# Packing two row blocks of w2 into each unit of the ternary weight passes, with the packed stores issued from SP

## The chip, the cores and the metric

The kernel runs on all 8 cores of one Trainium2 chip. Every core runs the same program on its own half of one sequence. The time is the device time of the slowest core in microseconds.

## What is computed

A layer in two parts, for x of shape (4, 4096, 1024). The first is a gated linear recurrence with projections and a layer norm. The second, which the change touches, is a feed-forward part with ternary weights ("bit linear") and a depthwise convolution of width 3 between its two products:

```python
def weight_quant(w):
    scale = 1.0 / jnp.clip(jnp.mean(jnp.abs(w)), 1e-05)
    return jnp.clip(jnp.round(w * scale), -1, 1) / scale

h = bit_linear(x, w1)                      # w1 (4096, 1024)
h = depthwise_conv1d(h.transpose(0, 2, 1), conv_w, conv_b)
h = jax.nn.silu(h.transpose(0, 2, 1))
return bit_linear(h, w2)                   # w2 (1024, 4096)
x = _layernorm(x + attn(x)); x = _layernorm(x + ffn(x))
```

So each weight matrix is read twice before it can be used: once for the mean of its absolute values, once to be scaled, rounded and clipped to -1, 0 or 1.

## The kernel before

Each core works on 2052 tokens (its 2048 and two on each side) in three stages that barriers separate (lines 665 and 1014).

Stage A prepares. Lines 336 to 415 fold the gate weights (`wtr`, `ps_pre`, `G`). The gate loop from line 574 then goes over all 4096 tokens in 16 slices of 256: SP loads `xgf` (1 MB in pieces of 1 KB, two buffers), ScalarE makes the high bf16 part `xgh`, GpSimd the low part `xgl`, TensorE does 24 matmuls into `ps_g`, and ScalarE writes three gate activations into `g80` (lines 601, 605, 609; `g` in the trace). A scan on VectorE (lines 636 and 641) gives the states.

The ternary work is woven into this stage. `tern_pass1` (line 437) takes a weight in units: a unit is a block of 128 rows by up to TW = 2048 columns in float32. w1, stored as (1024, 4096), gives 16 units of 1 MB. w2, stored as (4096, 1024), gives 32 units of 0.5 MB. Each unit is loaded by SP into one of four buffers `twf0` to `twf3`. Even units are summed by ScalarE (line 447), odd ones by VectorE (line 452). `pump_p1(9)` (line 612) advances this by nine units at the end of each gate slice, and since every engine runs its instructions in the order of the program, the loads of nine units stand ahead of the next slice's `xgf` on SP, and the sums stand between two slices' activations on ScalarE.

`tern_pass2` (line 486) runs after the scan, in the same units and buffers, w1 first. Of an even unit ScalarE makes `tu` (line 521, scaled), VectorE `tk16` (line 525, clamped to a 16-bit integer, `tk` in the trace), ScalarE `tb` (line 528, bf16). Of an odd unit VectorE makes `tu` and `tk16` (lines 532, 536) and ScalarE `tb` (line 539). There are two `tb` buffers. The store of `tb` to `w1q_hbm` or `w2q_hbm` is issued by ScalarE's queue, since that is the default of `store`:

```python
def load(dst_ap, src_ap, region, q="SP", reads=()):
def store(dst_ap, src_ap, reads, region, q="ACT"):
```

Waits come from `finalize_and_emit` (line 54): each operation names the regions that it reads and writes, and the engine waits, ahead of the instruction and in its own order, for the semaphores of the last writer and of the readers. A load into `twf0` therefore waits for whoever read `twf0` last, and a store waits for the cast that wrote its `tb`.

After the scan the kernel emits `tern_p2_all()` (line 662) and a barrier. Stage B (from line 667) first loads W_in, W_D and W_out in 24 pieces of 0.5 MB through two buffers `xb0` and `xb1`, with rows of 4 KB as those of w2, splits them in bf16 parts, then runs the projections (`ps_a`). Stage C is the feed-forward part (`ps_m`, `ps_o`), which reads `w1q_hbm` and `w2q_hbm`.

Of the kernel before, what the change touches and what calls it, by code (L numbers as in the profile page):

```python
# [184 lines left out]
def build_nc(debug=False):  # L185
    nc = bass.Bass("TRN2", target_bir_lowering=False)
    p = Prog(nc)
    V, A, PE, GP, SY = nc.vector, nc.scalar, nc.tensor, nc.gpsimd, nc.sync
# [53 lines left out]
    def load(dst_ap, src_ap, region, q="SP", reads=()):  # L242
        p.op(q, lambda d=dst_ap, s=src_ap, e=QENG[q]: e.dma_start(out=d, in_=s),
             reads=reads, writes=(region,), dma=True)

    def store(dst_ap, src_ap, reads, region, q="ACT"):
        p.op(q, lambda d=dst_ap, s=src_ap, e=QENG[q]: e.dma_start(out=d, in_=s),
             reads=reads, writes=(region,), dma=True)
# [32 lines left out]
    TW = 1024 if SAFE_ROUND else 2048  # L281
# [54 lines left out]
    for fc in range(8):  # L336
# [3 lines left out]
        for j in range(8):  # L340
# [6 lines left out]
             writes=(f"G{fc}",))  # L347
# [82 lines left out]

    twfs, tus, tk16s, tbs, tk, trr, tcp, tcol = alloc_tern(stA)

    def tern_slices(nrows, width):
        return [(rc, c0, min(width, c0 + TW))
                for rc in range(nrows) for c0 in range(0, width, TW)]

    def tern_pass1(src, nrows, width, mean_out, mean_rg, tg,
                   ps_hbuf, ps_rg, scol):
        stag = f"tcol{scol}"
        slices = tern_slices(nrows, width)  # L440
        for i, (rc, c0, c1) in enumerate(slices):
            wv = c1 - c0
            pr = i % NTB
            twf, tu = twfs[pr], tus[pr]
            load(twf[:, 0:wv], src[rc * 128:(rc + 1) * 128, c0:c1], f"twf{pr}")
            if i % 2 == 0:
                p.op("ACT", lambda twf=twf, tu=tu, e=wv: A.activation(
                    tu[:, 0:e], twf[:, 0:e], AF.Abs, accum_out=tcol[:, 0:1]),
                     reads=(f"twf{pr}",), writes=(f"tu{pr % 2}", "tcol0"))
                acc, arg = "tcol0", 0  # L450
            else:
                p.op("DVE", lambda twf=twf, e=wv: V.tensor_reduce(
                    tcol[:, 3:4].rearrange("p (t o) -> p t o", o=1),
                    twf[:, 0:e].rearrange("p (t e) -> p t e", t=1),
                    AX, OP.add, apply_absolute_value=True),
                     reads=(f"twf{pr}",), writes=("tcol3",))
                acc, arg = "tcol3", 3
            if i == 0:
                p.op("DVE", lambda: V.tensor_copy(tcol[:, 1:2], tcol[:, 0:1]),
                     reads=(acc,), writes=("tcol1",))  # L460
            else:
                p.op("DVE", lambda a=arg: V.tensor_add(tcol[:, 1:2],
                                                       tcol[:, 1:2],
                                                       tcol[:, a:a + 1]),
                     reads=(acc, "tcol1"), writes=("tcol1",))
            yield
        p.op("DVE", lambda: V.tensor_scalar(tcol[:, 1:2], tcol[:, 1:2],
                                            1.0 / (nrows * 128 * width), None,
                                            OP.mult),
             reads=("tcol1",), writes=("tcol1",))  # L470
        mm("parsum" + tg, ps_hbuf[0:1, 0:1], s_onesc[:], tcol[:, 1:2],
           reads=("s_onesc", "tcol1"), wr=ps_rg, start=True, stop=True)
        p.op("DVE", lambda: V.tensor_copy(tcol[0:1, 1:2], ps_hbuf[0:1, 0:1]),
             reads=(ps_rg,), writes=("tcol1",))
        mm("parbc" + tg, ps_hbuf[0:128, 0:1], s_ones1[:], tcol[0:1, 1:2],
           reads=("s_ones1", "tcol1"), wr=ps_rg, start=True, stop=True)
        p.op("DVE", lambda: V.tensor_copy(tcol[:, 1:2], ps_hbuf[0:128, 0:1]),
             reads=(ps_rg,), writes=("tcol1",))
        p.op("DVE", lambda: V.tensor_scalar_max(mean_out[:], tcol[:, 1:2], 1e-5),
             reads=("tcol1",), writes=(mean_rg,))  # L480
        p.op("DVE", lambda mo=mean_out, sc=scol: V.reciprocal(
            tcol[:, sc:sc + 1], mo[:]),
             reads=(mean_rg,), writes=(stag,))
        yield

    def tern_pass2(src, dst_hbm, nrows, width, tg, scol):
        stag = f"tcol{scol}"
        slices = tern_slices(nrows, width)
        for i, (rc, c0, c1) in enumerate(slices):
            wv = c1 - c0  # L490
            pr = i % NTB
            twf, tu, tk16, tb = twfs[pr], tus[pr], tk16s[pr], tbs[pr]
            load(twf[:, 0:wv], src[rc * 128:(rc + 1) * 128, c0:c1], f"twf{pr}")
            if SAFE_ROUND:
                p.op("DVE", lambda twf=twf, tu=tu, e=wv: V.tensor_scalar(
                    tu[:, 0:e], twf[:, 0:e], tcol[:, scol:scol + 1], None,
                    OP.mult),
                     reads=(f"twf{pr}", stag), writes=(f"tu{pr % 2}",))
                p.op("DVE", lambda tu=tu, e=wv: V.tensor_copy(tk[:, 0:e],
                                                              tu[:, 0:e]),  # L500
                     reads=(f"tu{pr % 2}",), writes=("tk",))
                p.op("DVE", lambda tu=tu, e=wv: V.tensor_sub(trr[:, 0:e],
                                                             tu[:, 0:e],
                                                             tk[:, 0:e]),
                     reads=(f"tu{pr % 2}", "tk"), writes=("trr",))
                p.op("DVE", lambda e=wv: V.tensor_scalar(tcp[:, 0:e], trr[:, 0:e],
                                                         0.5, None, OP.is_gt),
                     reads=("trr",), writes=("tcp",))
                p.op("DVE", lambda tu=tu, e=wv: V.scalar_tensor_tensor(
                    tu[:, 0:e], trr[:, 0:e], -0.5, tcp[:, 0:e], OP.is_lt,  # L510
                    OP.subtract),
                     reads=("trr", "tcp"), writes=(f"tu{pr % 2}",))
                p.op("DVE", lambda tu=tu, e=wv: V.tensor_sub(tu[:, 0:e],
                                                             tk[:, 0:e],
                                                             tu[:, 0:e]),
                     reads=(f"tu{pr % 2}", "tk"), writes=(f"tu{pr % 2}",))
                p.op("DVE", lambda tu=tu, tb=tb, e=wv: V.tensor_scalar(
                    tb[:, 0:e], tu[:, 0:e], 1.0, -1.0, OP.min, OP.max),
                     reads=(f"tu{pr % 2}",), writes=(f"tb{pr % 2}",))
            elif i % 2 == 0:  # L520
                p.op("ACT", lambda twf=twf, tu=tu, e=wv: A.activation(
                    tu[:, 0:e], twf[:, 0:e], AF.Identity,
                    scale=tcol[:, scol:scol + 1]),
                     reads=(f"twf{pr}", stag), writes=(f"tu{pr % 2}",))
                p.op("DVE", lambda tu=tu, tk16=tk16, e=wv: V.tensor_scalar(
                    tk16[:, 0:e], tu[:, 0:e], 1.49, -1.49, OP.min, OP.max),
                     reads=(f"tu{pr % 2}",), writes=(f"tk16{pr % 2}",))
                p.op("ACT", lambda tk16=tk16, tb=tb, e=wv: A.activation(
                    tb[:, 0:e], tk16[:, 0:e], AF.Copy),
                     reads=(f"tk16{pr % 2}",), writes=(f"tb{pr % 2}",))  # L530
            else:
                p.op("DVE", lambda twf=twf, tu=tu, e=wv: V.tensor_scalar(
                    tu[:, 0:e], twf[:, 0:e], tcol[:, scol:scol + 1], 1.49,
                    OP.mult, OP.min),
                     reads=(f"twf{pr}", stag), writes=(f"tu{pr % 2}",))
                p.op("DVE", lambda tu=tu, tk16=tk16, e=wv: V.tensor_scalar(
                    tk16[:, 0:e], tu[:, 0:e], -1.49, None, OP.max),
                     reads=(f"tu{pr % 2}",), writes=(f"tk16{pr % 2}",))
                p.op("ACT", lambda tk16=tk16, tb=tb, e=wv: A.activation(
                    tb[:, 0:e], tk16[:, 0:e], AF.Copy),  # L540
                     reads=(f"tk16{pr % 2}",), writes=(f"tb{pr % 2}",))
            store(dst_hbm[rc * 128:(rc + 1) * 128, c0:c1], tb[:, 0:wv],
                  (f"tb{pr % 2}",), f"q{tg}{rc}_{c0}")
            yield

    def tern_p1_all(ps_hbuf, ps_rg):
# [1056 lines left out]
```

How the kernel before makes its waits and increments, by code:

```python
                def body(handle, eng=eng, idxs=idxs):  # L164
                    for i in idxs:
                        o = ops[i]
                        for sh, val in waits_l[i]:
                            handle.wait_ge(sh, val)
                        instr = o["fn"]() if o["fn"] is not None else handle.nop()
                        if o["sem"] is not None:
                            instr.then_inc(o["sem"][1], 16 if o["dma"] else 1)
                    if eng == "SP":
                        for e2 in ENGINES:
                            if cnt.get(e2, 0):
                                handle.wait_ge(chain[e2], cnt[e2])
                        for j in range(NDMA):
                            if dcnt[j]:
                                handle.wait_ge(dpool[j], dcnt[j])
```

## Time and profile before

| what | us |
|---|---|
| median of three runs | 2483.28 (2475.99 to 2513.78) |
| the profiled execution, its own time | 2478.09 |
| its span, slowest core | 2476.6 |
| spans of all eight cores | 2451.3 to 2476.6 |
| pass 1 of both weights, within the gate slices | about 123 to 303 |
| pass 2 of w1, then of w2 | 459 to 551, 551 to 648 |
| first matmul of stage B | 756 |

The span is the time from the first instruction to the last on one core; the execution's own time is 1.5 us more. Times in the rows below count from the span's start. A row of instructions gives busy time and the idle time of the engine just before, with what ended it. "SPq" and "ACTq" are the queues' issues of a transfer. "Landing" is from the issue of a transfer to its completion.

### The profile page before, as it was taken

How to read it: one execution, taken by the hardware profiler on the slowest of the kernel's cores; microseconds unless marked ns; L12 is line 12 of the kernel's file. 1: busy time of each engine (PE TensorE's matmuls, PEld its weight loads, DVE VectorE, ACT ScalarE, POOL GpSimd, SP SyncE). 2: the span in 40 equal slices, each digit the busy share in tenths (PEclk: the TensorE clock that was granted, in tenths of full speed). 3: DMA queues.
4: the chain of work that ended last, by engine and by line, in shares of the span. 5: the costliest groups of instructions: out<-in, count | busy, mean ns of one | idle time of the engine just before them, and what ended most of it. 6: DMA issues, size and time to landing. Idle time of an engine off the chain costs nothing.

```text
span 2476.6 us, 30490 instructions; the slowest of 8 cores (2451.3 to 2476.6 us)
## 1 busy us (share of the span) xinstructions
PE 1343.5 (54%) x9255; PEld 965.8 (39%) x9255; DVE 1086.4 (44%) x2418; ACT 870.8 (35%) x1552; POOL 194.9 (8%) x78
## 2 busy tenths in 40 slices
PE   6712234000007786786886882056658568576566
PEld 6711133000006665665665762034335344343332
DVE  1123300433212433434334334278787787776852
ACT  0023322255311222122222221066465474574551
POOL 0011132000250001001001001000000000000000
PEclk9975566555558988998998986588879889788788
DMA  4385632587542101101100001450110110111000
GB/s 127 101 267 192 220 85 56 182 282 261 169 131 48 39 26 44 39 35 47 40 35 31 22 22 43 159 161 1 29 48 18 34 52 18 35 38 31 26 35 26
DMA packets 132968, 201.71 MB, mean 81 GB/s; under 512 B 46184, under 2 KB 95465, under 8 KB 127624
## 3 DMA queue, kind: packets, MB, share of 16 engines
q1 hardware_dynamic: 114120, 144.92, 20.0%
q10 hardware_dynamic: 18688, 54.85, 6.1%
q8 instruction: 78, 1.28, 0.2%
q14 instruction: 82, 0.67, 0.1%
HBM read 152.52 MB, written 38.03 MB: 77 GB/s over the span
## 4 chain that ended last, share of the span: by engine, by line
PE 35%; DVE 21%; DMA 15%; ACT 13%; issue 8%; POOL 6%; SPq 2%; ACTq 1%; DVEq 1%; POOLq 0%
PE ps_a L261 16%; PE ps_o L261 8%; DVE pmax L1337 5%; PE ps_m L261 4%; PE ps_g L261 3%; DMA xgf<-xg_fm 3%; POOL xgl L584 3%; DMA w2q_hbm<-tb 2%; DMA w1q_hbm<-tb 2%; PE ps_pre L261 2%; ACT sc_a L1088 2%; DVE hbuf L1311 2%; DVE sc_a L1106 2%; POOL xtm L893 2%; DMA wtr<-W_B_T 1%
## 5 line engine op out<-in xcount | busy, mean ns | idle before, releaser
L261 PE MATMUL ps_a<-pA_h,Win_hi 128*128 128x256 bf16 (+1 forms) x512 | 149.2, 291 | 403.9 <-ACT pA_h L739 329.5
L261 PE MATMUL ps_m<-r1qg,w1q 128*128 128x258 bf16 (+2 forms) x2304 | 301.9, 275 | 109.4 <-DVE hbuf L1311 69.6
L261 PE MATMUL ps_o<-w2q,hq_b 128*128 128x512 bf16 (+1 forms) x1088 | 288.6, 402 | 43.8 <-DVE ps_s L1433 23.6
L261 PEld LDWEIGHTS ps_m<-r1qg,w1q 128*128 128x128 bf16 x2304 | 212.8, 102 | 213.4 <-issue 147.2
L1088 ACT ACTIVATE sc_a<-hbuf,s_convb,s_convw 128x256 f32<-128x256 f32 (+2 forms) x288 | 166.1, 577 | 339.6 <-DVE hbuf L1311 319.2
L261 PEld LDWEIGHTS ps_a<-pA_h,Win_hi 128*128 128x128 bf16 x512 | 52.8, 103 | 420.8 <-issue 411.5
L261 PE MATMUL ps_a<-pB_h,WD_hi 128*128 128x256 bf16 (+1 forms) x512 | 148.4, 290 | 56.8 <-ACT pB_h L765 37.7
L261 PEld LDWEIGHTS ps_o<-w2q,hq_b 128*128 128x128 bf16 (+1 forms) x1088 | 106.5, 101 | 149.4 <-issue 67.7
L261 PE MATMUL ps_a<-pA_l,Win_hi 128*128 128x256 bf16 (+1 forms) x512 | 148.9, 291 | 6.9 <-DVE pA_l L743 6.9
L1311 DVE SCALAR_TENSOR_TENSOR hbuf<-ps_m,dqs 128x258 f32<-128x258 f32 (+2 forms) x288 | 113.1, 393 | 86.8 <-PE ps_m L261 81.7
L261 PE MATMUL ps_a<-pB_l,WD_hi 128*128 128x256 bf16 (+1 forms) x512 | 148.2, 289 | 1.1 <-DVE pB_l L769 1.1
L261 PE MATMUL ps_a<-pA_h,Win_lo 128*128 128x256 bf16 (+1 forms) x512 | 148.3, 290 | 0.0
L261 PE MATMUL ps_a<-pB_h,WD_lo 128*128 128x256 bf16 (+1 forms) x512 | 147.5, 288 | 0.0
L261 PE MATMUL ps_a<-pA_h,Wout_hi 128*128 128x256 bf16 (+1 forms) x512 | 139.4, 272 | 2.8 <-DVE zS L829 2.8
L261 PE MATMUL ps_a<-pA_l,Wout_hi 128*128 128x256 bf16 (+1 forms) x512 | 139.5, 272 | 0.0
L261 PE MATMUL ps_a<-pA_h,Wout_lo 128*128 128x256 bf16 (+1 forms) x512 | 139.0, 272 | 0.0
L1106 DVE SCALAR_TENSOR_TENSOR sc_a<-hbuf,s_convw,sc_a 128x256 f32<-128x256 f32 (+2 forms) x288 | 129.0, 448 | 15.9 <-ACT sc_a L1088 15.5
L1094 ACT ACTIVATE sc_d<-hbuf,s_convw 128x256 f32<-128x256 f32 (+2 forms) x288 | 135.5, 471 | 0.1
L261 PE MATMUL ps_g<-xgh,WG_hi 128*80 128x256 bf16 x128 | 51.6, 403 | 143.3 <-ACT xgh L580 143.3
L1114 DVE TENSOR_TENSOR sc_d<-sc_d,sc_a 128x256 f32<-128x256 f32 (+2 forms) x288 | 114.1, 396 | 30.6 <-DVE sc_a L1106 0.5
L1337 DVE TENSOR_REDUCE pmax<-hbuf 128x256 f32<-128x8192 f32 (+1 forms) x9 | 124.1, 13787 | 0.4 <-ACT hbuf L1118 0.4
L1118 ACT ACTIVATE hbuf<-sc_d 128x256 f32<-128x256 f32 (+2 forms) x288 | 112.8, 392 | 5.4 <-DVE sc_d L1114 4.7
(196 smaller groups left out, 2318.6 us busy)
## 6 DMA issues: line engine op xcount, KB each, us to landing
twf<-w1t_f SPq DMA_DIRECT2D x32, 1024.0 KB, 10.7
twf<-w2t_f SPq DMA_DIRECT2D x64, 512.0 KB, 5.4
xgf<-xg_fm SPq DMA_DIRECT2D x16, 1024.0 KB, 7.6
wtr<-W_B_T SPq DMA_DIRECT2D x16, 512.0 KB, 4.3
w1q_hbm<-tb ACTq DMA_DIRECT2D x16, 512.0 KB, 6.0
w2q_hbm<-tb ACTq DMA_DIRECT2D x32, 256.0 KB, 3.7
xtm<-x_tm ACTq DMA_DIRECT2D x16, 512.0 KB, 3.3
r_hbm<-z_tm ACTq DMA_DIRECT2D x16, 512.0 KB, 2.6
```

Source lines behind the costliest of these rows:

```text
L261: PE.matmul(o, l, r, start=st, stop=sp),
L584: GP.tensor_sub(xgl[:], xgf[:], xgh[:]),
L893: p.op("GP", lambda e=uw: GP.tensor_add(xtm[0:e, :], xtm[0:e, :], s_betb[0:e, :]), reads=("xtm", "s_betb"), writes=("xtm",))
L1088: A.activation(sc_as[mm_ % 2][:, 0:e], h[:, c0:c0 + e], AF.Identity, bias=s_convb[:, mm_:mm_ + 1], scale=s_convw[:, 32 + mm_:33 + mm_]),
L1094: A.activation(sc_ds[mm_ % 2][:, 0:e], h[:, c0 + 1:c0 + 1 + e], AF.Identity, scale=s_convw[:, 64 + mm_:65 + mm_]),
L1106: V.scalar_tensor_tensor(sc_as[mm_ % 2][:, 0:e], h[:, c0 - 1:c0 - 1 + e], s_convw[:, mm_:mm_ + 1], sc_as[mm_ % 2][:, 0:e], OP.mult, OP.add),
L1114: V.tensor_add(sc_ds[mm_ % 2][:, 0:e], sc_ds[mm_ % 2][:, 0:e], sc_as[mm_ % 2][:, 0:e]),
L1118: A.activation(h[:, c0:c0 + e], sc_ds[mm_ % 2][:, 0:e], AF.Silu),
L1311: V.scalar_tensor_tensor(o, i, 1.0, d, OP.mult, OP.mult),
L1337: p.op("DVE", lambda e=fw, c0=co: V.tensor_reduce(pmax[:, 0:e].rearrange("p (t o) -> p t o", o=1), hbuf[:, :].rearrange("p (c t) -> p t c" ...
```

## The change

`tern_slices` is replaced by `tern_units`. For w1 (4096 wide) nothing is different: a unit is 128 rows by 2048 columns. For w2 (1024 wide) a unit now has two blocks of 128 rows side by side in the buffer, 128 x 2 x 1024, so that both passes go over 16 units of 1 MB where there were 32 of 0.5 MB. All operations on such a unit are 2048 wide. Its load is one transfer of 1 MB in rows of 4 KB. Its store is one transfer of 0.5 MB in rows of 2 KB, and it is issued by SP (line 469 of the changed kernel), in the order of the program: behind the load of the same unit and ahead of the load of the next. The stores of w1 stay on ScalarE's queue.

```diff
--- before.py
+++ after.py
@@ -430,19 +430,53 @@
-    def tern_slices(nrows, width):
-        return [(rc, c0, min(width, c0 + TW))
-                for rc in range(nrows) for c0 in range(0, width, TW)]
+    def tern_units(srcT, nrows, width, tg, dstT=None):
+        units = []
+        if width >= TW:
+            for rc in range(nrows):
+                for c0 in range(0, width, TW):
+                    c1 = min(width, c0 + TW)
+                    sap = srcT[rc * 128:(rc + 1) * 128, c0:c1]
+                    dap = (None if dstT is None
+                           else dstT[rc * 128:(rc + 1) * 128, c0:c1])
+                    units.append((sap, dap, c1 - c0, None,
+                                  (f"q{tg}{rc}_{c0}",)))
+        else:
+            g = TW // width
+            for r0 in range(0, nrows, g):
+                ge = min(g, nrows - r0)
+                sap = srcT[r0 * 128:(r0 + ge) * 128, :].rearrange(
+                    "(c p) t -> p c t", p=128)
+                dap = (None if dstT is None
+                       else dstT[r0 * 128:(r0 + ge) * 128, :].rearrange(
+                           "(c p) t -> p c t", p=128))
+                units.append((sap, dap, ge * width, ge,
+                              tuple(f"q{tg}{r}_0" for r in range(r0, r0 + ge))))
+        return units
+
+    def tern_load(buf, sap, wv, gpack, region):
+        if gpack is None:
+            load(buf[:, 0:wv], sap, region)
+        else:
+            d3 = buf[:, 0:wv].rearrange("p (c t) -> p c t", c=gpack)
+            load(d3, sap, region)
+
+    def tern_store(buf, dap, wv, gpack, tags, rdtag):
+        if gpack is None:
+            store(dap, buf[:, 0:wv], (rdtag,), tags[0])
+        else:
+            s3 = buf[:, 0:wv].rearrange("p (c t) -> p c t", c=gpack)
+            p.op("SP", lambda d=dap, b=s3: SY.dma_start(out=d, in_=b),
+                 reads=(rdtag,), writes=tags, dma=True)
...
-        slices = tern_slices(nrows, width)
-        for i, (rc, c0, c1) in enumerate(slices):
-            wv = c1 - c0
+        units = tern_units(src, nrows, width, tg)
+        for i, (sap, dap, wv, gpack, tags) in enumerate(units):
             pr = i % NTB
             twf, tu = twfs[pr], tus[pr]
-            load(twf[:, 0:wv], src[rc * 128:(rc + 1) * 128, c0:c1], f"twf{pr}")
+            tern_load(twf, sap, wv, gpack, f"twf{pr}")
...
-            store(dst_hbm[rc * 128:(rc + 1) * 128, c0:c1], tb[:, 0:wv],
-                  (f"tb{pr % 2}",), f"q{tg}{rc}_{c0}")
+            tern_store(tb, dap, wv, gpack, tags, f"tb{pr % 2}")
             yield
```

(`tern_pass2` takes its units and its load in the same way as `tern_pass1`.)

SP's order in pass 2 of w2, before; a name's number is that of the buffer, and what stands in brackets are the semaphores that the engine waits for (`ch_ACT` and `ch_DVE` are the compute semaphores of ScalarE and VectorE, `dma...` those of transfers):

```order
L243 DMA twf3<-w2t_f 128x1024 [waits dma22,ch_DVE]
L243 DMA twf0<-w2t_f 128x1024 [waits dma24,ch_ACT]
L243 DMA twf1<-w2t_f 128x1024 [waits dma26,ch_DVE]
L243 DMA twf2<-w2t_f 128x1024 [waits dma28,ch_ACT]
L243 DMA twf3<-w2t_f 128x1024 [waits dma30,ch_DVE]
L243 DMA twf0<-w2t_f 128x1024 [waits dma0,ch_ACT]
```

And now:

```order
L243 DMA twf1<-w2t_f 128x2x1024
L469 DMA w2q_hbm<-tb1 128x2x1024 [waits ch_ACT]
L243 DMA twf2<-w2t_f 128x2x1024
L469 DMA w2q_hbm<-tb0 128x2x1024 [waits ch_ACT]
L243 DMA twf3<-w2t_f 128x2x1024
L469 DMA w2q_hbm<-tb1 128x2x1024 [waits ch_ACT]
L243 DMA twf0<-w2t_f 128x2x1024
L469 DMA w2q_hbm<-tb0 128x2x1024 [waits ch_ACT]
```

Each load was followed by the next load, four ahead. Now a store that waits for ScalarE stands between each load and the next, and the load itself has no wait of its own left.

ScalarE's order at the start of pass 2 of w2, before:

```order
L521 ACTIVATE tu0<-twf0,tcol 128x1024 [waits dma24]
L528 ACTIVATE tb0<-tk16_0 128x1024 [waits dma21,ch_DVE]
L247 DMA w2q_hbm<-tb0 128x1024 [waits ch_ACT]
L539 ACTIVATE tb1<-tk16_1 128x1024 [waits dma23,ch_DVE]
L247 DMA w2q_hbm<-tb1 128x1024 [waits ch_ACT]
L521 ACTIVATE tu0<-twf2,tcol 128x1024 [waits dma28]
L528 ACTIVATE tb0<-tk16_0 128x1024 [waits dma25,ch_DVE]
```

And now (lines 554, 561 and 572 are the former 521, 528 and 539):

```order
L554 ACTIVATE tu0<-twf0,tcol 128x2048 [waits dma8]
L561 ACTIVATE tb0<-tk16_0 128x2048 [waits dma5,ch_DVE]
L572 ACTIVATE tb1<-tk16_1 128x2048 [waits dma7,ch_DVE]
L554 ACTIVATE tu0<-twf2,tcol 128x2048 [waits dma12]
L561 ACTIVATE tb0<-tk16_0 128x2048 [waits dma9,ch_DVE]
```

The two stores in each pair are gone from its queue, and `tu` and `tb` are 2048 wide.

SP's order in pass 1, from the first unit of w2 to the second `xgf` after it, before and now:

```order
L243 DMA twf0<-w2t_f 128x1024 [waits dma0,ch_ACT]
L256 DMA xgf0<-xg_fm 128x8x256
L243 DMA twf1<-w2t_f 128x1024 [waits dma1,ch_DVE]
L243 DMA twf2<-w2t_f 128x1024 [waits dma2,ch_ACT]
L243 DMA twf3<-w2t_f 128x1024 [waits dma3,ch_DVE]
L243 DMA twf0<-w2t_f 128x1024 [waits dma4,ch_ACT]
L243 DMA twf1<-w2t_f 128x1024 [waits dma6,ch_DVE]
L243 DMA twf2<-w2t_f 128x1024 [waits dma7,ch_ACT]
L243 DMA twf3<-w2t_f 128x1024 [waits dma8,ch_DVE]
L243 DMA twf0<-w2t_f 128x1024 [waits dma9,ch_ACT]
L243 DMA twf1<-w2t_f 128x1024 [waits dma10,ch_DVE]
L256 DMA xgf1<-xg_fm 128x8x256
```

```order
L243 DMA twf0<-w2t_f 128x2x1024 [waits dma0,ch_ACT]
L256 DMA xgf0<-xg_fm 128x8x256
L243 DMA twf1<-w2t_f 128x2x1024 [waits dma1,ch_DVE]
L243 DMA twf2<-w2t_f 128x2x1024 [waits dma2,ch_ACT]
L243 DMA twf3<-w2t_f 128x2x1024 [waits dma3,ch_DVE]
L243 DMA twf0<-w2t_f 128x2x1024 [waits dma4,ch_ACT]
L243 DMA twf1<-w2t_f 128x2x1024 [waits dma6,ch_DVE]
L243 DMA twf2<-w2t_f 128x2x1024 [waits dma7,ch_ACT]
L243 DMA twf3<-w2t_f 128x2x1024 [waits dma8,ch_DVE]
L243 DMA twf0<-w2t_f 128x2x1024 [waits dma9,ch_ACT]
L243 DMA twf1<-w2t_f 128x2x1024 [waits dma10,ch_DVE]
L256 DMA xgf1<-xg_fm 128x8x256
```

The order is the same, with units of twice the size. Before, 22 units were left after these; now 6 are.

## Rows read from the trace of the kernel before

**Rows 1.** The page, part 4 (chain by line) and part 5 (costliest groups)

```profile
PE ps_a L261 16%; PE ps_o L261 8%; DVE pmax L1337 5%; PE ps_m L261 4%; PE ps_g L261 3%; DMA xgf<-xg_fm 3%; POOL xgl L584 3%; DMA w2q_hbm<-tb 2%; DMA w1q_hbm<-tb 2%; PE ps_pre L261 2%; ACT sc_a L1088 2%; DVE hbuf L1311 2%; DVE sc_a L1106 2%; POOL xtm L893 2%; DMA wtr<-W_B_T 1%
...
L261 PE MATMUL ps_a<-pA_h,Win_hi 128*128 128x256 bf16 (+1 forms) x512 | 149.2, 291 | 403.9 <-ACT pA_h L739 329.5
```

**Rows 2.** Busy time by stretch (start:end, then its length), pass 1, pass 2, stage B loads

```profile
core 5: us, PE busy (x) PEld busy (x) DVE busy (x) ACT busy (x) POOL busy (x), PEclk, DMA share, GB/s
...
147.90:188.80 40.90, 5.50 (x24) 4.34 (x24) 14.01 (x15) 13.34 (x15) 4.06 (x1) 0.54 0.82 282
188.80:217.20 28.40, 5.87 (x28) 4.82 (x28) 13.36 (x17) 10.47 (x12) 4.05 (x1) 0.58 0.64 222
...
271.90:299.30 27.40, 4.92 (x24) 4.02 (x24) 6.00 (x12) 7.90 (x12) 4.05 (x1) 0.56 0.81 268
299.30:314.90 15.60, 6.20 (x28) 4.95 (x28) 3.75 (x11) 5.55 (x10) 4.05 (x1) 0.54 0.24 68
314.90:326.90 12.00, 4.65 (x24) 3.82 (x24) 0.00 (x0) 3.26 (x4) 4.05 (x1) 0.61 0.25 64
459.00:544.30 85.30, 0.00 (x0) 0.00 (x0) 25.66 (x22) 42.77 (x22) 0.00 (x0) 0.50 0.91 291
551.00:648.10 97.10, 0.00 (x0) 0.00 (x0) 32.80 (x48) 51.84 (x48) 0.00 (x0) 0.50 0.75 246
648.10:756.00 107.90, 0.15 (x1) 0.10 (x1) 12.23 (x13) 13.39 (x15) 50.86 (x24) 0.50 0.50 131
```

**Rows 3.** The chain in order of time, end of pass 2 (start, length, what)

```profile
632.78 5.15 DMA w2q_hbm<-tb
638.07 1.07 ACT tb L528
...
646.04 2.03 DMA w2q_hbm<-tb
```

**Rows 4.** SP's own waits between 551 and 648 us (total, times, longest)

```profile
SPq L168 <- ACT tu L521: 58.3, 14, 5.2
SPq L168 <- DVE tu L532: 14.0, 14, 1.0
```

**Rows 5.** Instructions in order of time, an odd unit of w1, then an even one

```profile
493.54 1.28 DVE L532 TENSOR_SCALAR tu<-twf,tcol 128x2048 f32<-128x2048 f32 x1
...
498.23 0.33 ACTq L247 DMA_DIRECT2D w1q_hbm<-tb  x1
...
542.18 2.00 ACT L521 ACTIVATE tu<-twf,tcol 128x2048 f32<-128x2048 f32 x1 [0.51 <-ACT tb L539]
544.26 2.86 SPq L243 DMA_DIRECT2D twf<-w2t_f  x2
...
545.61 1.91 ACT L528 ACTIVATE tb<-tk 128x2048 bf16<-128x2048 int16 x1 [1.43 <-DVE tk L525]
...
547.60 0.33 ACTq L247 DMA_DIRECT2D w1q_hbm<-tb  x1
548.13 1.91 ACT L539 ACTIVATE tb<-tk 128x2048 bf16<-128x2048 int16 x1 [0.62 <-DVE tk L536]
```

**Rows 6.** DMA issues with size and median us to landing: pass 2, weight loads, page

```profile
twf<-w1t_f SPq DMA_DIRECT2D x16, 1024.0 KB, 10.7
...
twf<-w2t_f SPq DMA_DIRECT2D x28, 512.0 KB, 5.1
...
xb<-W_D SPq DMA_DIRECT2D x8, 512.0 KB, 4.4
xb<-W_in SPq DMA_DIRECT2D x6, 512.0 KB, 4.1
...
r_hbm<-z_tm ACTq DMA_DIRECT2D x16, 512.0 KB, 2.6
```

**Rows 7.** Tile xgf between 320 and 420 us, one 1 MB load at a time

```profile
DMA to landing us min/median/max: 5.6/7.0/7.6
```

**Rows 8.** The chain in order of time, a 512 KB weight load of stage B

```profile
655.80 3.74 DMA xb<-W_in
```

More of the change, by code:

```diff
@@ L487, in tern_pass2 @@
         stag = f"tcol{scol}"
-        slices = tern_slices(nrows, width)
-        for i, (rc, c0, c1) in enumerate(slices):
-            wv = c1 - c0
+        units = tern_units(src, nrows, width, tg, dstT=dst_hbm)
+        for i, (sap, dap, wv, gpack, tags) in enumerate(units):
             pr = i % NTB
             twf, tu, tk16, tb = twfs[pr], tus[pr], tk16s[pr], tbs[pr]
-            load(twf[:, 0:wv], src[rc * 128:(rc + 1) * 128, c0:c1], f"twf{pr}")
+            tern_load(twf, sap, wv, gpack, f"twf{pr}")
             if SAFE_ROUND:
```

## The prediction

> **What bounds the kernel now.** I read the page's chain that ended last first, to see whether the ternary weight work is on it at all: the stores `w2q_hbm<-tb` and `w1q_hbm<-tb` hold 2% of the span each [rows 1]. The costliest group of matmuls then shows what their stage means for TensorE: its first `ps_a` matmul sat 329.5 us behind `pA_h` [rows 1]. In all of that time TensorE does nothing, because the barrier after pass 2 lets no weight of stage B load before the last store of `w2q_hbm` has landed. So a microsecond in pass 2 is a microsecond of the kernel.
>
> Next, busy time by stretch [rows 2]. Pass 2 of w2 takes 97.1 us (551.0 to 648.1) with ScalarE busy 51.8 and VectorE 32.8 and the DMA engines 75%: 16.8 MB in and 8.4 MB out at 246 GB/s. Pass 2 of w1 takes 85.3 us up to 544.3 at 291 GB/s. No engine is full; loads run four buffers ahead. The chain in pass 2 of w2 alternates ScalarE casts with landings of stores [rows 3], which is a loop over the two `tb` buffers with transfers kept in flight. SP's own waits in that stretch are for the reader that frees a `twf` buffer [rows 4], never for the data of a store: those are ACT's.
>
> In pass 1 I cut at the ends of the gate activations: 147.9, 188.8, 217.2, 244.5, 271.9, 299.3, 314.9, 326.9 us. The stretch after a slice's gates, up to the next slice's, took 40.9 us with 9 units of w1 (1 MB each), 28.4 with 7 of w1 and one of w2, 27.4 with 9 of w2 (0.5 MB; there are three of these, the first 27.3), 15.6 with the last four, and 12.0 with none [rows 2].
>
> **The change, part by part.**
>
> Pass 1 of w2: 32 units become 16. The bytes stay. The third and fourth stretch now carry 9 and 6 units of 1 MB, and the fifth and sixth none. I price each by the stretch with about the same bytes, and half a megabyte more at 291 GB/s at 1.8 us: 40.9 + (28.4 + 1.8) + 40.9 + (28.4 + 1.8) + 12.0 + 12.0 = 166.2 us, against 314.9 - 147.9 = 167.0 before. I take 0. Bounds: if half of the added megabytes hid under the matmuls of a slice, the 40.9 us of the third slice would be 27.4, so -13; if the fourth went at the pace of the first (40.9 x 7/9 = 31.8) and the empty ones took 15.6, +8.
>
> Pass 2 of w2, compute: two 1024-wide instructions become one 2048-wide, for the cast 2 x 1.07 us against 1.91 [rows 3, 5]. Over 24 pairs ScalarE saves 24 x 0.23 = 5 us of its 51.8, and it is not what limits. Pass 1 saves 8 such pairs on ScalarE beside transfers: nothing.
>
> Pass 2 of w2, queue: this decides. The store moves from ACT's queue to SP's and stands between the load of its own unit and the load of the next. SP is in order. So behind the waiting store all later loads are queued, and ScalarE waits for these. The load of unit i+1 is issued only when unit i has been loaded, scaled, clamped and cast: the four buffers are of no more use, and one load is in flight at a time. Period of a unit:
>
> (a) from landing to the issue of the store. An even unit of this width: `tu` starts 542.18, store issued 547.60: 5.4 us. An odd one: `tu` starts 493.54, store issued 498.23: 4.7 us [rows 5]. Mean 5.05, taken as 5.1.
>
> (b) SP issues the store, then the load: 0.33 us of issue as in the store's row [rows 5], so the load is issued 0.4 us after the store.
>
> (c) the load, alone in its queue but for the store ahead of it. No row of before has that. From below: 512 KB of the same 4 KB rows took 5.1 us with others in flight, and 4.1 to 4.4 nearly alone [rows 6]. From above: 1 MB amid other loads and stores took 10.7 [rows 6]. Between: 1 MB alone in 1 KB pieces took 5.6 to 7.6, median 7.0 [rows 7]. I build it as 4.3 for the first half megabyte, 1.8 for the second at 291 GB/s, and half of the 1.8 that the store's 512 KB would need ahead of it: 7.0 us.
>
> Period 5.1 + 0.4 + 7.0 = 12.5 us, where before 97.1 / 16 = 6.1 us moved the same megabyte. Start: the first w2 load is issued at 544.26 as now (it waits for unit 12 of w1, [rows 5]); in the tail of w1's traffic I give it 8.3 us, landing at 552.6, after ScalarE is through with w1 (548.13 + 1.91 = 550.0, [rows 5]). Its store is issued 0.1 + 5.4 us later, at 558.1. Fifteen more periods: 745.6. The last store, 512 KB, lands in 2.6 us, as the 512 KB stores of r1 do [rows 6]: 748.2. Now it lands at 646.04 + 2.03 = 648.1 [rows 3]. Loss: 100 us. With (c) at 5.1 the period is 10.6 and the loss 72; with 10.7 it is 16.2 and 156.
>
> What speaks against this is a rule on queues. SP's 58.3 + 14.0 us of waiting on readers [rows 4] show that a wait holds back what is queued behind it, and here the new wait is for the end of a chain. The Trainium skill (DMA: Bandwidth & Descriptors, Issuing engines are not separate DMA queues) says that transfers from SP and ACT share the same 16 engines, and that spreading them over issuers saves only the time to initiate. By that the move would be free. It speaks of transfers; the trace shows what waits ahead of an issue do, and I go by the trace.
>
> A second rule is for larger transfers. In traffic 512 KB took 5.1 us and 1 MB 10.7 [rows 6], so a megabyte costs 10.2 as two and 10.7 as one: nothing is won. The Trainium skill (DMA: Bandwidth & Descriptors, Bandwidth: Measured) advises transfers of at least 1 MiB to reach 75% of peak; with several in flight the trace does not bear out a gain. The same page's fit (Anatomy of one DMA) of 2.0 us plus bytes at 436 GB/s gives, as an estimate, 4.4 us for a lone 1 MB load; with it in (c), and no share for the store, the loss would be 61 us.
>
> Stage B and the FFN: same instructions, later by the same amount. The granted clock is 0.50 all through pass 2 and the weight loads [rows 2], so a longer idle cannot lower it further.
>
> Sum: the profiled execution took 2478.1 us (span 2476.6). 2478.1 + 100 + 0 = 2578. It lies 5.2 below the median of three runs; I add 2 for that: 2580.
>
> **The rivals.**
>
> *Quick loads.* With seven other cores also loading half the time, a lone megabyte lands in 5.1 us: period 10.6, loss 72, time 2550. For: the DMA engines were 75% busy and will be under half. Against: even 512 KB nearly alone took 4.1 to 4.4.
>
> *Slow loads.* The store's writes hold the load behind them in the same queue, and (c) is 10.7 as in traffic: loss 156, time 2634. Against: that row has four loads ahead of it.
>
> *Not slower: the queue does not hold.* If the store's wait kept no load back, the stage would be bound by its transfers. At the 291 GB/s of w1's stretch the 25.2 MB take 86.5 us, 11 less than now: 2467, within 2%. It decides from a period of (648.1 + 50 - 2.6 - 558.1) / 15 = 9.2 us down, that is a load of at most 3.7 us; 3.74 is the shortest I see for half the bytes [rows 8]. Also the queue's order after the change leaves no load to be issued ahead of the wait. So it is nearly excluded.
>
> *Pass 1 moves it.* Its bounds of -13 and +8 widen the range and decide no sign.
>
> **How the numbers follow.** Forecast, a load of 5.5 to 8.6 us: 0.80. Quick loads 0.08, slow loads 0.08, not slower 0.04. A measurement of this kernel tells about 2% (50 us) from no change; the first three cases lie over it, so slower 0.96, within 2% 0.03, faster 0.01 (only the last case, helped by pass 1 and more). Range: load 5.5 gives a period of 11.0 and a loss of 78, with -7 from pass 1: 2550. Load 8.6 gives 14.1 and 124, with +8: 2612.
>
> **What would show it.** In the changed trace: SP waits for ACT `tb` before each of 16 stores, some 12 us each; ScalarE idles before `tu` on a landing of `twf<-w2t_f`, 16 times by about 7 us; landings of these loads in pass 2 near 7 us; DMA share between 552 and 748 near 0.4; the gates end where they do now, within 10 us. The forecast is wrong if two w2 loads are in flight at once in pass 2, if the stage ends before 700, or if the time after it differs by more than 10 us from now.

## The result, and the profile after

The changed kernel takes 2557.3 us in the median of nine runs (2553.4 to 2614.1) against 2485.1 us before (ten runs, 2476.0 to 2548.5). The ratio is 1.030, 95% interval 1.028 to 1.031: slower by some 74 us. Some executions of every kernel here ran slower with one half of the chip at a lower clock (the upper ends of the ranges); the ratios leave them out. Forecast were 2580 us and a range of 2550 to 2612.

The profiled execution took 2559.1 us, its span is 2557.5 us, on core 2 (that of before was on core 5). Answering to [rows 1], the page's chain by line and its costliest group; lines of the file are 32 higher behind the new functions:

```profile
PE ps_a L261 17%; PE ps_o L261 8%; DVE pmax L1369 5%; PE ps_m L261 4%; DMA twf<-w2t_f 4%; PE ps_g L261 3%; DMA xgf<-xg_fm 3%; POOL xgl L616 3%; PE ps_pre L261 2%; DVE sc_a L1138 2%; DMA w1q_hbm<-tb 2%; DVE hbuf L1343 2%; ACT sc_a L1120 2%; DMA wtr<-W_B_T 2%; POOL xtm L925 1%
...
L261 PE MATMUL ps_a<-pA_h,Win_hi 128*128 128x256 bf16 (+1 forms) x512 | 148.3, 290 | 484.6 <-ACT pA_h L771 411.4
```

TensorE now sits 411.4 us behind `pA_h` where it sat 329.5, 82 us more; the loads `twf<-w2t_f` are on the chain with 4%, and `w2q_hbm<-tb`, 2% before, is no longer among the first.

The chain in order of time, in pass 2 of w2 (start, length, what; pieces under 0.1 us left out), which answers to [rows 3]:

```profile
619.13 5.65 DMA twf<-w2t_f
...
624.87 1.30 DVE tu L565
626.27 1.24 DVE tk L569
627.59 1.92 ACT tb L572
629.57 0.37 SPq L469
629.98 6.04 DMA twf<-w2t_f
636.10 2.01 ACT tu L554
638.21 1.24 DVE tk L558
639.53 1.92 ACT tb L561
641.51 0.37 SPq L469
641.92 6.03 DMA twf<-w2t_f
```

This is the whole loop, an odd unit and an even one: load, scale, clamp, cast, issue of the store, next load. Only the landing of the store runs beside it; no two loads are in flight together. From the landing of the odd load (619.13 + 5.65 = 624.78) to the issue of its store are 4.8 us, of the even one (636.02 to 641.51) 5.5; the next load is issued 0.4 us behind the store. The first store was issued at 549.84, the last at 723.81: 15 periods of 11.6 us.

SP's own waits in that stretch, against [rows 4], and the landings (KB, median us), against [rows 6]:

```profile
SPq L168 <- ACT tb L561: 101.2, 8, 22.2
SPq L168 <- ACT tb L572: 80.9, 8, 10.7
```

```profile
twf<-w2t_f SPq DMA_DIRECT2D x15, 1024.0 KB, 5.9
w2q_hbm<-tb SPq DMA_DIRECT2D x15, 512.0 KB, 3.3
```

Sixteen waits for the cast, of 11.4 us each in the mean (a third row of that view is one wait of 2.3 us behind the last store); no reader of a `twf` is waited for any more. Busy time by stretch, against [rows 2]:

```profile
core 2: us, PE busy (x) PEld busy (x) DVE busy (x) ACT busy (x) POOL busy (x), PEclk, DMA share, GB/s
...
188.80:223.20 34.40, 5.39 (x28) 4.43 (x28) 11.13 (x17) 11.32 (x13) 4.06 (x1) 0.55 0.80 274
223.20:259.90 36.70, 5.43 (x24) 4.34 (x24) 10.31 (x12) 11.29 (x13) 4.05 (x1) 0.53 0.77 258
259.90:286.10 26.20, 6.25 (x28) 4.97 (x28) 8.48 (x14) 9.28 (x10) 4.06 (x1) 0.53 0.61 200
286.10:298.20 12.10, 4.67 (x24) 3.84 (x24) 0.00 (x0) 3.30 (x4) 4.05 (x1) 0.61 0.30 87
...
549.80:723.80 174.00, 0.00 (x0) 0.00 (x0) 28.68 (x23) 42.64 (x22) 0.00 (x0) 0.50 0.41 136
```

The DMA engines are at 41% and 136 GB/s, where they were at 75% and 246. In pass 1 the stretches are 40.9, 34.4, 36.7, 26.2, 12.1 and 12.9 us, 163.2 in all against 167.0.

Since the slowest core differs from run to run, I took three lengths on each of the eight cores from the views of the tiles, for every kernel of this study. Medians over the cores, in us: the gates from the first slice's activation to the last slice's (pass 1 lies in it), pass 2 of both weights from the first store of w1q to the first load of W_in, and from there to the end:

| kernel | gates | pass 2 | the rest | ratio to before, 95% interval |
|---|---|---|---|---|
| before | 277.2 | 176.4 | 1820.1 | 1 |
| changed | 270.6 | 257.8 | 1824.8 | 1.030 (1.028 to 1.031) |
| pack_act | 270.6 | 159.8 | 1825.0 | 0.991 (0.988 to 0.994) |
| split_sp | 276.8 | 310.0 | 1822.1 | 1.060 (1.054 to 1.066) |
| pack_sp_ahead | 272.4 | 156.9 | 1822.0 | 0.990 (0.986 to 0.993) |
| wait_only | 272.3 | 258.1 | 1824.8 | 1.032 (1.028 to 1.036) |
| pass1_only | 271.7 | 176.6 | 1820.3 | 0.996 (0.995 to 0.998) |
| pack_act_4tb | 270.6 | 144.6 | 1821.9 | 0.984 (0.982 to 0.985) |
| split_act_4tb | 276.3 | 152.4 | 1820.4 | 0.991 (0.988 to 0.994) |
| load_alone | 269.6 | 279.6 | 1824.5 | 1.041 (1.039 to 1.043) |

The change costs 81 us in pass 2 and gives back 7 in pass 1. The rest is 5 us longer. Each length is from one profiled execution of a kernel, so they do not add up exactly to the 74 us of the ratio.

### The profile page after: what moved, and what is told of

The parts are those of the page before. It is cut to its first block, busy times and chain, and to the rows that moved or that the text cites. A ratio compares the mean times of both kernels' runs of the same rounds, so it can differ in the third digit from the quotient of the medians.

```text
span 2557.5 us, 30049 instructions; the slowest of 8 cores (2527.8 to 2557.5 us)
## 1 busy us (share of the span) xinstructions
PE 1346.0 (53%) x9210; PEld 968.1 (38%) x9255; DVE 1072.9 (42%) x2370; ACT 861.5 (34%) x1512; POOL 194.9 (8%) x78
## 4 chain that ended last, share of the span: by engine, by line
PE 35%; DVE 21%; DMA 16%; ACT 13%; issue 7%; POOL 6%; SPq 2%; DVEq 1%; ACTq 0%; POOLq 0%
PE ps_a L261 17%; PE ps_o L261 8%; DVE pmax L1369 5%; PE ps_m L261 4%; DMA twf<-w2t_f 4%; PE ps_g L261 3%; DMA xgf<-xg_fm 3%; POOL xgl L616 3%; PE ps_pre L261 2%; DVE sc_a L1138 2%; DMA w1q_hbm<-tb 2%; DVE hbuf L1343 2%; ACT sc_a L1120 2%; DMA wtr<-W_B_T 2%; POOL xtm L925 1%
## 5 line engine op out<-in xcount | busy, mean ns | idle before, releaser
L261 PE MATMUL ps_a<-pA_h,Win_hi 128*128 128x256 bf16 (+1 forms) x512 | 148.3, 290 | 484.6 <-ACT pA_h L771 411.4
L261 PE MATMUL ps_o<-w2q,hq_b 128*128 128x512 bf16 (+1 forms) x1043 | 283.3, 405 | 47.4 <-DVE ps_s L1465 23.3
## 6 DMA issues: line engine op xcount, KB each, us to landing
twf<-w1t_f SPq DMA_DIRECT2D x32, 1024.0 KB, 11.4
```

The source lines that it names most:

```text
L261: PE.matmul(o, l, r, start=st, stop=sp),
```

## Experiments

**pack_act: the packing without the move to SP.** The only edit to the changed kernel:

```diff
-            p.op("SP", lambda d=dap, b=s3: SY.dma_start(out=d, in_=b),
+            p.op("ACT", lambda d=dap, b=s3: A.dma_start(out=d, in_=b),
```

> Packed units as in the change, but the packed store is issued by ScalarE's queue as before. Theory A (the loss is SP's wait for the cast, which keeps the next load back): pass 2 of w2 back at 88 to 98 us, pass 1 some 5 us shorter as in the changed kernel, so 0 to 12 us below the kernel before (about 2470 to 2485). Theory B (the packing itself costs, by transfers of 1 MB and less overlap): it stays 40 us or more above before. Theory C (half and half): 20 to 40 above.

Measured: 0.991 of before, some 22 us faster. Pass 2 falls from 257.8 to 159.8, so the move to SP, in this order of loads and stores, costs 98 us. The stores of w2q, by their issues:

```profile
L469 ACTq DMA_DIRECT2D w2q_hbm<-tb x16: 366/366/377, 555.3 to 627.2; - x16
```

(627.2 - 555.3) / 15 = 4.8 us for a unit, against 11.6. Theories B and C are out. The gain was larger than theory A had allowed (12 us at most): packing is worth 17 us in pass 2, which I come back to below.

**split_sp: the move to SP without the packing.** With the first edit every unit of w2 is 0.5 MB again, in both passes; with the second its stores still go by SP:

```diff
-        if width >= TW:
+        if True:
...
-            tern_store(tb, dap, wv, gpack, tags, f"tb{pr % 2}")
+            store(dap, tb[:, 0:wv], (f"tb{pr % 2}",), tags[0],
+                  q="SP" if tg == "w2" else "ACT")
```

> Units of 0.5 MB as before in both passes, but w2's stores are issued by SP between the loads. Theory A: the period of a unit is a chain of about 3.1 us (half widths), 0.4 for SP and a lone load of 4.0 to 4.6 us, so 7.5 to 8.1 us, 32 times: 240 to 260 us for pass 2 of w2 against 97, the kernel about 150 us above before (some 2630). Theory B: no loss, as nothing is packed (within 10 us of before).

Measured: 1.060, some 148 us slower, as theory A had it. Instructions in order of time, one period:

```profile
606.37 0.33 SPq L247 DMA_DIRECT2D w2q_hbm<-tb  x1
606.75 0.42 SPq L243 DMA_DIRECT2D twf<-w2t_f  x1
610.81 1.15 ACT L554 ACTIVATE tu<-twf,tcol 128x1024 f32<-128x1024 f32 x1 [4.51 <-DMA twf<-w2t_f]
...
612.85 1.06 ACT L561 ACTIVATE tb<-tk 128x1024 bf16<-128x1024 int16 x1 [0.89 <-DVE tk L558]
613.97 0.33 SPq L247 DMA_DIRECT2D w2q_hbm<-tb  x1
```

From store to store 7.6 us, with a load landing about 4.1 us after its issue. Half the bytes in each period cost well over half the period. That the packed kernel loses only half as much is thus owed to its packing.

**pack_sp_ahead: stores on SP, behind later loads.** The load of unit i+3 is put ahead of unit i's store; all stores stay on SP:

```diff
-            tern_load(twf, sap, wv, gpack, f"twf{pr}")
+            if tg == "w1":
+                tern_load(twf, sap, wv, gpack, f"twf{pr}")
+            else:
+                for j in (range(0, 4) if i == 0 else (i + 3,)):
+                    if j < len(units):
+                        s_, _, w_, g_, _ = units[j]
+                        tern_load(twfs[j % NTB], s_, w_, g_,
+                                  f"twf{j % NTB}")
```

> Packed, stores on SP, but the load of unit i+3 is put ahead of the store of unit i in the order of the program, so that three or four loads stay in flight. Theory A (the order on SP, not the queue as such): pass 2 of w2 at 88 to 102 us, the kernel within 12 us of before. Theory D (SP as issuer of both, one queue for loads and stores, is the cost): it stays 40 us or more above before.

Measured: 0.990, 25 us faster than before, and as fast as with the stores on ScalarE's queue. The gain was again larger than expected (within 12 us), as in pack_act. Theory D is out: SP can issue both. What is issued in SP's queue:

```profile
563.75 0.37 SPq L469 DMA_DIRECT2D w2q_hbm<-tb  x1
564.16 0.47 SPq L243 DMA_DIRECT2D twf<-w2t_f  x1
566.16 0.37 SPq L469 DMA_DIRECT2D w2q_hbm<-tb  x1
566.57 0.52 SPq L243 DMA_DIRECT2D twf<-w2t_f  x1
571.38 0.37 SPq L469 DMA_DIRECT2D w2q_hbm<-tb  x1
571.79 0.48 SPq L243 DMA_DIRECT2D twf<-w2t_f  x1
```

Store and load still alternate, but the load behind a store belongs to a unit four further on than the store's, so that the wait for a cast no longer stands between a load and its use. It is the order that costs, not the queue.

**wait_only: the wait without the store in the queue.** Stores on ScalarE's queue as in pack_act, and each load reads the `tb` of the unit before:

```diff
-            tern_load(twf, sap, wv, gpack, f"twf{pr}")
+            if tg == "w1" or i == 0:
+                tern_load(twf, sap, wv, gpack, f"twf{pr}")
+            else:
+                d3 = twf[:, 0:wv].rearrange("p (c t) -> p c t", c=gpack)
+                load(d3, sap, f"twf{pr}", reads=(f"tb{(i - 1) % 2}",))
```

> Packed, stores on ScalarE's queue, but each w2 load in pass 2 waits for the cast of the unit before, by a read of its tb. This has the wait without the store ahead of the load in SP's queue. Theory A (the wait alone): period 11.0 to 11.6 us against 11.6 in the changed kernel, the loss against before 64 to 78 us. Theory E (a good part of the 5.9 us of the load is the store ahead of it in the same queue): loads near 4.6 us, period near 10, the loss 45 to 55 us.

Measured: 1.032, 79 us slower, 1 us over the upper end of theory A, with pass 2 at 258.1 us against 257.8 in the changed kernel. The wait reproduces the loss with no store in the queue of the loads. The 4.6 us of theory E do not appear; the landings go the other way:

```profile
twf<-w2t_f SPq DMA_DIRECT2D x14, 1024.0 KB, 6.5
w2q_hbm<-tb ACTq DMA_DIRECT2D x14, 512.0 KB, 6.9
```

With the store issued at the same moment on another queue the load takes 6.5 us instead of 5.9, and the store 6.9 instead of 3.3; the 0.4 us saved on SP are lost again. So the queue that the store stands in does not make the loss. What a store in flight costs the load, wherever it was issued, this run cannot tell, since the store still runs beside the load; the next one can.

**load_alone: load and store each alone.** Stores on ScalarE's queue as in pack_act; the load waits until the store of the unit before has landed:

```diff
...
+                load(d3, sap, f"twf{pr}", reads=units[i - 1][4])
```

> Packed, stores on ScalarE's queue, and each w2 load in pass 2 waits until the store of the unit before has landed, so that load and store are each alone. Measures term (c) without a store ahead. If the store costs the load its share as in the prediction (0.9 us), the load lands in 5.0 us; if little, in 5.7 or more. Period 5.2 + store 2.6 to 3.3 + load: 13.0 to 14.3 us, the kernel about 95 to 115 us above before.

Measured: 1.041, about 102 us slower. The landings:

```profile
twf<-w2t_f SPq DMA_DIRECT2D x12, 1024.0 KB, 4.9
w2q_hbm<-tb ACTq DMA_DIRECT2D x13, 512.0 KB, 3.1
```

With no other transfer of this core's stage in flight a megabyte lands in 4.9 us; the 5.9 of the changed kernel are 1.0 more, which is what the store just ahead of it in SP's queue costs it. (The other seven cores run the same stage in both.) This takes term (c) of the prediction into its two parts.

**pass1_only: packing in pass 1 alone.**

```diff
-        if width >= TW:
+        if width >= TW or dstT is not None:
```

> Only pass 1 of w2 is packed; pass 2 is that of the kernel before. From the changed kernel's trace pass 1 should give 4 us: 2 to 6 us below before, ratio 0.997 to 0.999. If the whole 22 us gain of the packed kernel with ScalarE's stores came from pass 1, it would be 0.991.

Measured: 0.996 (0.995 to 0.998), that is 9 us with an interval of 5 to 12, more than the 2 to 6 expected, though the interval reaches into them. In the traces the gates take 5.5 us less, and pass 2 and the rest are as before. Pass 1 is not where the packed kernel's 22 us come from, only part of them.

**split_act_4tb and pack_act_4tb: four `tb` buffers.** The question was why packing gains in pass 2. ScalarE's waits for landings of stores, in the kernel before, from 455 to 640 us:

```profile
ACT tb L528 <- DMA w1q_hbm<-tb: 19.7, 5, 5.7
ACT tb L528 <- DMA w2q_hbm<-tb: 19.7, 10, 2.8
ACT tb L539 <- DMA w1q_hbm<-tb: 6.3, 3, 3.3
```

With two `tb` buffers a cast cannot start before the store of two units ago has landed. In both kernels the two `xgh` buffers, idle by then, serve as the third and fourth `tb` (the cut lines put `TB` in place of the old name where the casts write and the store reads):

```diff
+        tb4 = (tbs[0], tbs[1], xghs[0], xghs[1])
+        tbr4 = ("tb0", "tb1", "xgh0", "xgh1")
...
-            twf, tu, tk16, tb = twfs[pr], tus[pr], tk16s[pr], tbs[pr]
+            twf, tu, tk16, tb = twfs[pr], tus[pr], tk16s[pr], tb4[pr]
+            TB = tbr4[pr]
...
```

> The kernel before with four tb buffers in pass 2 and nothing else. Theory F: the stretch of w2 falls from 98 to 82 to 90 us, so the kernel is 8 to 16 us below before; packing gained by needing half as many landings. Theory H (larger transfers are cheaper in themselves): the stretch stays at 95 to 98 us, the kernel within 4 us of before.

> Packed, stores on ScalarE's queue, and four tb buffers in pass 2 (the two xgh buffers serve as the third and fourth). Theory F (in the kernel before pass 2 is held by the landing of stores behind two tb buffers): ScalarE's waits for the landing of stores go, the stretch of w2 goes from 84 to 78 to 82 us and that of w1 falls by 0 to 6, so 4 to 12 us below the two-buffer version, about 2452. Theory G (it is bound by transfers): no difference over 3 us.

Measured: the unpacked one 0.991 (some 22 us faster than before), with pass 2 at 152.4 against 176.4; the packed one 0.984 (some 40 us), with pass 2 at 144.6 against 159.8. Both gained more than expected. No wait for a landed store is left in either; the longest waits of pack_act_4tb between 455 and 605 us are for other engines' work and one for loads of w1:

```profile
DVE tk L561 <- ACT tu L557: 82.8, 16, 11.4
ACT tu L557 <- DMA twf<-w1t_f: 14.2, 4, 11.7
ACT tb L575 <- DVE tk L572: 11.8, 8, 2.7
ACT tb L564 <- DVE tk L561: 11.4, 8, 1.4
```

Theory F holds: the kernel before was held in pass 2 by landings of stores behind two buffers. Over pass 2 of both weights four buffers without packing gain more (24 us) than packing with two (17). But the buffers serve w1 too, which packing leaves alone. Two more lengths from the same views, medians over the cores in us, part the weights:

| kernel | first to last store of w1 | last store of w1 to first load of W_in |
|---|---|---|
| before | 75.6 | 100.5 |
| pack_act | 77.6 | 82.4 |
| split_act_4tb | 65.6 | 85.7 |
| pack_act_4tb | 65.5 | 78.6 |

In w2 alone packing takes 18 us and the buffers 15; the other 10 of the buffers are w1's. With four buffers packing still takes 7 us in w2. So of packing's 18 us some 11 are no longer there to be had once the buffers are enough, which fits fewer landings to wait for, and 7 have another cause, which no run looked for. pack_act_4tb beats both kernels of this case, at 2438.8 us.

## Why the prediction was right

The sign, the place and the mechanism were right, and the sizes of three terms were not: the loop of load, compute, cast, store and next load on SP, one load in flight. The runs take it apart in both directions (pack_act and pack_sp_ahead remove it, wait_only and split_sp make it).

By its own steps:

- (a), landing to store: forecast 5.1, measured (4.8 + 5.5) / 2 = 5.1. Right.
- (b), 0.4: measured 0.41. Right.
- (c), the load: forecast 7.0, measured 5.9 in the median of the landings, 6.1 by the period (11.6 less 5.1 and 0.4). This term was too large. load_alone shows where: the share of the store was priced at 0.9 and is 1.0; the lone megabyte was priced at 6.1 (4.3 + 1.8) and is 4.9. Which of its two halves was too high is not shown, since no run has a lone half megabyte in pass 2. The 4.3 came from loads of stage B, where [rows 8] has 3.74 as well; the 291 GB/s behind the 1.8 is the rate of a stretch with several transfers competing. Over 15 periods the 0.9 us are some 14 us.
- The start: the first w2 store was forecast for 558.1 and came at 549.84. Of the 8.3 us, 4.2 lie before pass 2 (its first load was issued at 454.85, not 459.07), 2.0 in pass 2 of w1 (from there to the end of its last cast, 89.0 against 91.0), and the remaining 2 are a misreading. I took the issues at 544.26 [rows 5] for the first of w2, but the view began behind the first one. SP's issues in a longer window, before and then in the changed kernel:

```profile
534.93 24.80 SPq L243 DMA_DIRECT2D twf<-w2t_f  x8
```

```profile
527.17 0.38 SPq L243 DMA_DIRECT2D twf<-w2t_f  x1
```

  The first w2 load was thus issued at 534.93, right behind the read of w1's unit 12, and its data were there when ScalarE was through with w1. Nothing was waited for at the start, and the 8.3 us that I gave this load had no place in the sum.
- The end of pass 2: 748.2 forecast, 726.5 measured (723.81 + 2.73 by the chain). The 8.3 of the start + 15 x 0.9 = 21.8 explains it.
- Pass 1, taken as 0: measured -7 between the medians of the cores, inside the bounds of -13 and +8. The stretch priced at 30.2 took 34.4, those priced at 40.9 and 30.2 took 36.7 and 26.2.
- "Nothing is won" by larger transfers: wrong. Packing is worth 17 us in pass 2 once the loads run ahead. I compared landing times per megabyte, but the stretch was held by the number of landings that two `tb` buffers allow, which the chain of [rows 3] showed and I had even called a loop. The 98 us that the move to SP costs against pack_act are near the 100 of my sum by chance only: my 100 was the loss against the kernel before, which is 81 in pass 2.
- The rest of the kernel, taken as equal: 1824.8 against 1820.1. It is within the 10 us that I had allowed.
- The range: 2557.3 lies 7 us above its lower end, at the quick loads' 2550, and 23 below the forecast. In (c) that rival (5.1 us) was as near to the truth as the forecast. All the misses, of the start, of (c) and of pass 1, go the same way. Slow loads are excluded by the landings of 5.9 us, and the queue that does not hold by SP's sixteen waits and by pack_act.

What stays open: the 2 to 5 us that the rest takes longer where pass 2 is packed, and in split_sp, and not in pass1_only or split_act_4tb. The cores of one execution differ by more than that (1816.0 to 1828.3 us before), so it may be nothing. No run was made for it.

## What to carry to other kernels

A queue that runs in order turns a store behind its cast into a gate for every load behind it: look at what stands behind a waiting instruction, not at which engine issues it, and if a queue has to carry both, put the loads of the next units ahead of the store. Moving or packing transfers can pay and lose at once; take the edit apart, since here its good half (22 us) was hidden behind 98 us of the bad one. And where casts wait for landed stores, count the buffers before the bytes: two more gained as much in the whole kernel as the packing (22 us each).

## What was not expected of the hardware

Three ways to run the same 1 MB load and 512 KB store gave these medians: each alone 4.9 and 3.1 us; the load 0.4 us behind the store in one queue 5.9 and 3.3; both at once from two queues 6.5 and 6.9. With the other cores at the same work, one queue kept the store nearly at its own price and made only the load pay; two queues let both pay, as the Trainium skill (DMA: Bandwidth & Descriptors, Issuing engines are not separate DMA queues) has it, that transfers of both issuers run on the same engines and interleave. The same page's fit (Anatomy of one DMA), which it gives for transfers issued by GpSimd and by which I had estimated 4.4 us for a lone megabyte, is nearer to the 4.9 of load_alone than the 6.1 that I had built from rows in traffic.
